# A denser interleave of attention and expert items (0.75 to 0.65 of the expert list), and hT loads in two halves, in a fused linear-attention and mixture-of-experts layer

## The reference, cut to what matters

```python
q, k, v = x @ Wq, x @ Wk, x @ Wv               # x after a layernorm, 4096 x 1024 per core
q = softmax(q over the 64 features of a head) * SCALE
k = softmax(k over the 4096 tokens)
context = einsum('bhdn,bhen->bhde', k, v)      # 64 x 64 per head, 8 heads
att = einsum('bhde,bhdn->bhen', context, q) @ Wo + bo
y = x + layernorm(att)
u = layernorm(y)
s = softmax(u @ centroids.T + expert_biases)   # 16 experts, the two largest kept as gates g
routed = sum over e of g[e] * (u @ Wr[e] + br[e])
shared = (u @ Ws[0] + u @ Ws[1] + bs) / 2
out = y + layernorm(u + routed + shared)
```

## Time and profile before

| what | us |
|---|---|
| median of 2 runs | 3082.54 (3076.98 to 3088.11) |
| the profiled execution, its time | 3076.98 |
| its span on the slowest core (core 2) | 3075.2 |
| spans of the 8 cores | 3054.6 to 3075.2 |
| PE busy | 2447.1 (80%) |
| DVE busy | 1575.1 (51%) |
| ACT busy | 113.0 (4%) |

### The profile page before, as it was taken

The page is one execution under the profiler, slowest core; times in us unless marked ns, Lnnn a source line. Parts: engine busy times, 40 slices in busy tenths (PEclk is TensorE's granted clock), DMA queues, the critical chain, the costliest instruction groups (busy, mean ns, idle before and its releaser), DMA issues.

```text
span 3075.2 us, 38404 instructions; the slowest of 8 cores (3054.6 to 3075.2 us)
## 1 busy us (share of the span) xinstructions
PE 2447.1 (80%) x12014; PEld 1107.6 (36%) x12014; DVE 1575.1 (51%) x2882; ACT 113.0 (4%) x353; POOL 15.8 (1%) x29
## 2 busy tenths in 40 slices
PE   3243521439999999499999994999999949999994
PEld 1121210114444444144444441444444414444442
DVE  4132321666566654566566445665664454444445
ACT  0000000000000000000000000000000000000000
POOL 0000000000000000000000000000000000000000
PEclk9666765569999999699999996999999979999997
DMA  5989898222354353433553545335434443343444
GB/s 110 130 131 149 146 133 126 69 69 64 72 106 104 69 110 73 142 78 67 104 107 64 109 78 142 76 68 105 103 69 86 78 139 64 75 79 75 78 76 133
DMA packets 673684, 296.32 MB, mean 96 GB/s; under 512 B 631857, under 2 KB 634929, under 8 KB 672340
## 3 DMA queue, kind: packets, MB, share of 16 engines
q1 hardware_dynamic: 668308, 251.86, 36.4%
q0 software_dynamic: 5184, 42.01, 11.5%
HBM read 142.78 MB, written 79.69 MB: 72 GB/s over the span
## 4 chain that ended last, share of the span: by engine, by line
PE 67%; DMA 11%; DVE 8%; SPq 4%; another core or an unknown queue 3%; DVEq 3%; issue 3%; ACT 0%; POOL 0%; ACTq 0%; POOLq 0%
PE pb L882 58%; DMA xA<-xin 8%; SPq L79 4%; PE pb L827 2%; PE pb L785 2%; PE pb L871 2%; DMA yld<-yscr 1%; DVEq L416 1%; DVE ftmp L628 1%; DMA cen_st<-cen 1%; DVE ftmp L625 1%; DVEq L64 1%; PE pbT L732 1%; DMA wrt<-wbf 1%
## 5 line engine op out<-in xcount | busy, mean ns | idle before, releaser
L882 PE MATMUL pb<-wrt,uT 128*128 128x512 bf16 x9216 | 2015.8, 379 | 3.5 <-DMA wrt<-wbf 2.2
L882 PEld LDWEIGHTS pb<-wrt,uT 128*128 128x128 bf16 x9216 | 893.3, 98 | 1072.8 <-issue 12.3
L602 DVE SCALAR_TENSOR_TENSOR racc<-pb,gAll,racc 128x512 f32<-128x512 f32 x1024 | 755.0, 750 | 793.0 <-PE pb L882 769.9
L732 PE MATMUL pbT<-eye,hb 128*128 128x128 bf16 x256 | 32.1, 306 | 219.7 <-DVEq L64 219.2
L602 DVE SCALAR_TENSOR_TENSOR racc<-pb,halfc,racc 128x512 f32<-128x512 f32 x128 | 96.1, 751 | 125.1 <-PE pb L882 125.1
L785 PE MATMUL pb<-wqb,hT 128*128 128x512 bf16 x256 | 70.4, 430 | 77.8 <-DMA hT<-hscr 77.8
L732 PEld LDWEIGHTS pbT<-eye,hb 128*128 128x128 bf16 x256 | 24.8, 137 | 225.8 <-issue 225.5
L414 DVE BATCH_NORM_STATS2 Abn<-xA 128x6 f32<-128x512 f32 x32 | 22.2, 693 | 137.9 <-DMA xA<-xin 134.4
L798 PE MATMUL pbT<-eye,qn 128*128 128x128 bf16 x128 | 13.5, 233 | 85.5 <-DVEq L64 85.4
L871 PE MATMUL pb<-eyeblk,uT 128*128 128x512 bf16 x256 | 77.9, 434 | 0.0
L453 DVE CAST vb<-pb 128x512 bf16<-128x512 f32 x32 | 22.2, 694 | 106.2 <-PE pb L759 81.3
(11 more groups left out here) (107 smaller groups left out, 913.1 us busy)
## 6 DMA issues: line engine op xcount, KB each, us to landing
xA<-xin SPq DMA_DIRECT2D x128, 256.0 KB, 6.0
wbf<-wr POOLq DMA_DIRECT2D x16, 2048.0 KB, 36.3
wrt<-wbf SPq DMA_TRANSPOSE x1152, 3.0
yscr<-att SPq DMA_DIRECT2D x32, 512.0 KB, 3.9
yld<-yscr SPq DMA_DIRECT2D x32, 512.0 KB, 4.2
out<-ftmp SPq DMA_DIRECT2D x32, 512.0 KB, 2.9
hscr<-hT SPq DMA_DIRECT2D x32, 256.0 KB, 37.1
hT<-hscr SPq DMA_DIRECT2D x32, 256.0 KB, 5.1
```

What stands on the lines that cost most here:

```text
L602: ii = v.scalar_tensor_tensor(rsl, pb[bk][:], gcol, rsl, ALU.mult, ALU.add)
L732: last = pe.transpose(pT[:, kk * P:(kk + 1) * P], hb4[i4][:, kk * P:(kk + 1) * P], eye[:])
L882: last = pe.matmul(pb[bk][:], uT[:, kk * NTOK + tt * P:kk * NTOK + (tt + 1) * P], wrt[par][:, kk * HID:(kk + 1) * HID], start=(kk == 0), s ...
```

## The change

The share of `lb` over which A2 is spread goes from 0.75 to 0.65. Each load of `hT` becomes two DMAs of half the columns, each with a semaphore of its own, and `a2_p_q` waits for both.

```diff
             outl.append(la[ia])
-            want = int(round((ia + 1) * ratio * 0.75))
+            want = int(round((ia + 1) * ratio * 0.65))
             while ib < want:
...
-                em.dma(sync, f"dHL{(t + 2) % 2}", t + 2, hT[(t + 2) % 2][:],
-                       hscr[(t + 2) * P:(t + 3) * P, :])
+                em.dma(sync, f"dHL{(t + 2) % 2}", t + 2,
+                       hT[(t + 2) % 2][:, 0:HID],
+                       hscr[(t + 2) * P:(t + 3) * P, 0:HID])
+                em.dma(sync, f"dHLh{(t + 2) % 2}", t + 2,
+                       hT[(t + 2) % 2][:, HID:D],
+                       hscr[(t + 2) * P:(t + 3) * P, HID:D])
...
             em.wait(pe, f"dHL{t % 2}", t)
+            em.wait(pe, f"dHLh{t % 2}", t)
...
-            em.dma(sync, f"dHL{c}", c, hT[c][:], hscr[c * P:(c + 1) * P, :])
+            em.dma(sync, f"dHL{c}", c, hT[c][:, 0:HID],
+                   hscr[c * P:(c + 1) * P, 0:HID])
+            em.dma(sync, f"dHLh{c}", c, hT[c][:, HID:D],
+                   hscr[c * P:(c + 1) * P, HID:D])
```

## The result

The changed kernel takes 3138.24 us (median of 13 runs) against 3090.4 us (median of 12 runs of the kernel before, the two shown earlier among them). The ratio is 1.0143, with a 95% interval of 1.0112 to 1.0175: 1.4% slower. The medians are over all runs; the ratio leaves out those in which the cores of one die showed a lower granted clock and a longer time, as happened now and then with either kernel. The forecast was 39 us more than the profiled execution before, given as a median of 3118 in the range 3078 to 3145. The profiled execution after took 3128.26 us with a span of 3126.6 on its slowest core, again core 2.

The account below looks back on a forecast made before the run. PE was taken to set the pace in the mixed rounds; 22 + 7 + 2 + 1 + 1 + 6 + 0 = 39 us on the profiled 3077.0 made 3116, given as 3118, range 3078 to 3145.

Parts of the forecast that it names:

- main case: Whole kernel: the added waits and clock falls come as summed, 3118 us, own range 3098 to 3135; chance 0.60.
- burst from att to ub: Mixed rounds 1 to 3: PE has fewer units to cover DVE's attention work and waits for ub; net +22 us.
- gates: Before the gate transposes: four units instead of five cover DVE's 8.5 us in more pairs; net +7 us, 4 to 12.
- q softmax: Up to the second qn: tiles 10/11 have three units as cover, 1.8 us late, tiles 12/13 lose 0.3; net +2 us.
- the first pair of round 1: There short bias units cover the q softmax; fewer of them make PE wait about 1 us more.
- starts of rounds 2 and 3: PE's first o2 starts 5.7 us earlier, but DVE's work up to ub stays; +1 us together, between -11 and +10.
- clock: After new waits over 2 us, half of seven bring a granted-clock fall costing 1.7 us each; +6 us, 0 to 12.
- hT halves: Loads of hT at phase one's end: the same bytes land in the same DMA drain, so 0 us.
- the rival: hT loads: second halves queue under the casts, price up to 39 us, 3155 us; chance 0.06.
- The faster case: Starts of rounds 2 and 3 each keep 5.7 us and the bursts are covered: 3066 us; chance 0.07.
- The case of no waits: Mixed rounds: DVE works through the burst faster, or PE's time between items is longer; 3077 to 3090 us; chance 0.15.
- at every one: All PE waits, short ones too: the clock falls each time, 1.7 us per fall; 3149 us; chance 0.12.

Follow-up runs that it names:

- 0.55: The kernel before with the share set to 0.55 and hT loads whole: ratio 1.0276, phase two 2641.4 us.
- 0.90: The kernel before with the share set to 0.90 and hT loads whole: ratio 0.9907, phase two 2541.6 us.
- the start version: Kernel before, share 0.75, with a quarter's first two yld loads ahead of its last weight transposes and the next quarter's bias units under the finals: ratio 0.9759.

## Why the prediction was right

Right in direction, in size and, step by step, mostly in composition. The median of 3138 lies in the range, but 20 us above the 3118 forecast and 3 above the 3135 that the prediction gave as its main case's own upper end. The profiled execution was 12 us over its forecast of 3116, and all of that is the later start of phase two, 526.7 instead of 514.5 us on core 2, which the forecast did not have. The forecast also stood on two runs; over twelve the median before is 8 us higher. From the first q matmul on, on core 2:

| step | predicted, us | measured, us |
|---|---|---|
| burst from att to ub, ten pairs | +22 (23.2 less 1.2) | +22 (23.5 less 1.3) |
| gates | +7 | +8 (12.6 less 4.6) |
| q softmax, and the first pair of round 1 | +2 and +1 | +1.4 |
| starts of rounds 2 and 3 | +1 | +0.6 |
| clock | +6 | about +5 |
| hT halves | 0 | 0 to +3 (phase two after, less that of the share alone) |
| sum; measured as a whole | +39 | +39.2 |

The burst came out pair by pair: 3.9 us at tiles 10/11 (predicted 4.1), then 2.3 and 2.2 (2.3, 2.3), 3.2, 2.2 and 1.1 in round 2 (3.0, 2.3, 1.3), 2.9, 2.6 and 1.0 in round 3 (the same three). Only tiles 8/9 were further off, 0.9 and 1.1 us in two waits for 1.3. That the burst is the cause is shown by shortening it: 2.4 us less of it per pair took 24.6 us of ub waits away at 0.65. That the sum holds elsewhere in total is shown by 0.55.

The starts were named as a gain of 5.7 us that is not kept, and it wasn't: PE's first o2 came 46.7 us after the q matmuls instead of 53.2, yet ub's transposes, less the units done, came after 77.5 us instead of 78.0, and in round 3 after 78.6 instead of 77.5. But I had one reason wrong. I took DVE's fixed work as the whole of it and did not see that the bias units ahead of o2 are work that can go under the finals. At 0.65 two things seem to cancel, earlier attention items and later bias units; no run has the one without the other. At 0.90 the starts came out shorter by 7.5 us in round 2 and 4.7 in round 3.

The clock term came out near by luck: it stood on three falls, not on half of seven, and two of the three were at waits that the sum did not count. In stretches of 15 us three behind the waits of a mixed stage show 0.89 where before such stretches were at 1.00: after the two waits of tiles 8/9, after the 3.94 us wait, and after the 2.39 us wait at the start of round 3. After the second, the lowered stretch is in the row above, 865 to 868 us at 0.50, the 1.2 GHz level, and sixteen matmuls that take 3.62 us at 1.00 took 5.30: 1.7 us per fall. The other six waits of the seven, 2.2 to 3.2 us in rounds 1 to 3, left the clock alone. The prediction took from the Trainium skill (TensorE: Matmul & The Clock Gate, HAM oscillation) that all seven would fall. The idle gaps that this section speaks of are longer than those six waits; behind the one wait that is long enough, 3.94 us, the clock did fall. So the prediction applied the section to gaps that it doesn't cover. The falls at tiles 8/9 and at the start of round 3 it doesn't cover either.

The hT halves are the weakest step. That the first hT doesn't come later for them held: its wait grew by 1.5 us, not by 39. But one reason was wrong: an issue does not cost 0.35 us everywhere. Under the casts one held SP for 16.2 us. No wait of PE came of it, since SP had waited 13.3 us for the last cast before its first weight transposes and waited 1.0 us now. That SP's later extra issues pass behind the units is not shown. At 0.75 they may cost 0 to 10 us through the weight transposes; at 0.65 phase two with halves is 1 to 3 us over the share alone. For the rival the prediction drew on the Trainium skill (DMA: Bandwidth & Descriptors, queues, rings and completion order), by which a DMA engine takes its queues in turn, packet by packet. A later first hT would have followed from turns lost to the casts; no run here shows it.

The faster case failed on both conditions: the starts kept none of the gain, and the bursts were not covered. The case of no waits failed at every pair, and the clock fell at three waits of the many, not at every one.

## What to carry to other kernels

Where two engines share one ordered list, an engine's mean load says little: DVE was at 62% and still held PE up, since its work came in bursts of 23 us that had to fit under what PE had between two items. So take the burst's work on the one side, count the other engine's units between the same items on the other, and do it pair by pair; with durations from one trace this gave nine of ten waits within 0.3 us, and the tenth within 0.8. And before changing how densely things are mixed, look where the idle time is: here it stood in three stretches of 40 us, and filling these with the next quarter's cheap units won twice what the density could.

## What was not expected

- PE's waits for weight transposes changed with the share: 2 to 6 us by core in the kernel before, 0 to 3.5 at 0.65, 4 to 10 at 0.90. It looks as if a wait taken from one place comes back in part at this one; the start version, with 3.1 us in the mean, does not fit that.
- The granted clock fell after a wait of 3.94 us and stayed up after one of 3.23, but it also fell after two waits of about 1 us each, 1.7 us apart, at tiles 8/9, with 24.5 us of weight matmuls ahead of them. What decides it is open.
- The start of phase two moved between 489 and 545 us over cores and executions, though phase one's own work is the same in every kernel. For a change of 1%, that part has to be taken off before two profiles are compared.
